# A sliding-window attention stage on one Trainium2 core: another way to the inverse norms, product runs in halves, and a new order on all engines

## What is computed

```
for i in range(6):                                   # DEPTH
    x = attn_layer(shift_tokens(x), ...) + x
    x = ffn_layer(shift_tokens(x), ...) + x
attn_layer:
    q, k, v = split(x @ Wqkv)                        # 16 heads of 64
    q = l2norm(q) * q_scale;  k = l2norm(k) * k_scale   # t / max(norm(t), 1e-12)
    q, k = rotary(q), rotary(k)                      # with tables of cosine, sine and scale
    sim = 8 * q k^T over windows of 32 and the window before, masked
    out = softmax(sim) @ v;  return out @ Wo
ffn_layer:
    xn = (x - mean) / sqrt(var + 1e-5) * g + b
    a, gate = split(xn @ W1 + b1)                    # 2 x 341
    return a * gelu(gate) @ W2 + b2
```

## Time and profile before

| | |
|---|---|
| median of three executions | 5155.24 us (5143.06 to 5160.82) |
| span of the profiled execution | 5148.7 us; its own device time is not listed apart and lies among those of the runs |
| TensorE | busy 4508.2 us, 88% |
| VectorE | busy 3456.9 us, 67% |
| GpSimd | busy 3075.1 us, 60% |
| ScalarE | busy 2317.0 us, 45% |
| mean granted TensorE clock | 0.910 over the span, 1.00 in the deep stage |

### The profile page before, as it was taken

One profiled execution on the slowest core, in us unless ns is written; L12 is line 12 of the kernel. 1 busy time (PEld: TensorE's weight loads), 2 busy tenths in 40 slices (PEclk: granted clock), 3 DMA queues, 4 the chain that ended last, 5 costly groups with the idle time before them and its releaser, 6 DMA issues.

```text
span 5148.7 us, 147111 instructions
## 1 busy us (share of the span) xinstructions
PE 4508.2 (88%) x66028; PEld 2555.2 (50%) x66028; DVE 3456.9 (67%) x4153; ACT 2317.0 (45%) x2523; POOL 3075.1 (60%) x1713
## 2 busy tenths in 40 slices
PE   6898689977468999999999999568999999999998
PEld 3444333333135555555555555235555555555554
DVE  4365536632437778778777776447877787888885
ACT  1242134433134555555555555234555555555553
POOL 0010000000019889888889997049988899998984
PEclk7699679976569999999999999669999999999999
DMA  2000000000001112111111111101111111112111
GB/s 71 1 1 1 0 0 1 1 0 0 0 22 32 30 29 55 29 51 32 52 29 53 31 29 33 44 9 29 33 51 30 35 49 30 54 29 55 30 32 29
DMA packets 78094, 144.43 MB, mean 28 GB/s; under 512 B 18728, under 2 KB 24944, under 8 KB 75824
## 3 DMA queue, kind: packets, MB, share of 16 engines
q1 hardware_dynamic: 77488, 135.23, 10.1%
HBM read 39.75 MB, written 1.05 MB: 8 GB/s over the span
## 4 chain that ended last, share of the span: by engine, by line
PE 47%; issue 23%; POOL 21%; DVE 7%; ACT 1%; DMA 0%; SPq 0%; DVEq 0%; POOLq 0%
POOL arena L1446 8%; PE psum L1033 8%; POOL arena L1439 6%; POOL arena L1452 5%; PE psum L1050 4%; PE psum L1064 4%; PE psum L1102 4%; PE psum L1083 4%; PE psum L1002 3%; PE psum L1148 3%; PE psum L1097 2%; PE psum L1142 2%; PE psum L524 2%; POOL rstd L1457 2%; PE psum L1016 2%
## 5 line engine op out<-in xcount | busy, mean ns | idle before, releaser
L1446 POOL TENSOR_TENSOR arena<-arena,minus_half 128x16 f32<-128x16 f32 x384 | 1131.9, 2948 | 32.0
L1439 POOL TENSOR_TENSOR arena<-arena 128x1024 f32<-128x1024 f32 x384 | 909.8, 2369 | 13.5 <-DVE arena L1324 13.5
L1452 POOL TENSOR_TENSOR arena<-arena 128x1024 f32<-128x1024 f32 x384 | 733.7, 1911 | 42.6
L1320 DVE TENSOR_TENSOR arena<-psum,arena 128x1024 f32<-128x1024 f32 x384 | 468.1, 1219 | 404.1 <-ACT arena L1202 404.1
L1462 POOL MEMSET arena<- 128x33 f32 x4 | 0.4, 128 | 995.3 <-DVE std L1686 995.3
L1208 ACT ACTIVATE arena<-psum 128x1024 f32<-128x1024 f32 x384 | 392.2, 1021 | 298.8 <-PE psum L1050 298.4
L1202 ACT ACTIVATE arena<-psum 128x1024 f32<-128x1024 f32 x384 | 392.3, 1022 | 246.5 <-PE psum L1033 243.4
L1324 DVE TENSOR_TENSOR arena<-psum,arena 128x1024 f32<-128x1024 f32 x384 | 466.8, 1215 | 54.1 <-PE psum L1050 54.1
L1050 PEld LDWEIGHTS psum<-w_ident,arena 128*128 128x128 f32 x3072 | 355.3, 141 | 281.9 <-issue 148.5
L1331 DVE TENSOR_REDUCE arena<-arena 128x16 f32<-128x1024 f32 x384 | 464.8, 1211 | 2.8
L1235 ACT ACTIVATE arena<-psum 128x1024 f32<-128x1024 f32 x192 | 196.7, 1024 | 580.7 <-PE psum L1064 580.7
(11 more groups left out here) (260 smaller groups left out, 7703.9 us busy)
## 6 DMA issues: line engine op xcount, KB each, us to landing
arena<-arena SPq DMA_DIRECT2D x672, 128.0 KB, 2.3
deep_wqkv<-in_deep_wqkv SPq DMA_DIRECT2D x6, 1536.0 KB, 7.1
arena<-in_deep_wqkv SPq DMA_DIRECT2D x6, 1536.0 KB, 7.2
arena<-arena SPq DMA_DIRECT2D x96, 64.0 KB, 2.5
deep_wo<-in_deep_wo SPq DMA_DIRECT2D x6, 512.0 KB, 7.5
arena<-in_deep_wo SPq DMA_DIRECT2D x6, 512.0 KB, 7.4
deep_w<-in_deep_w SPq DMA_DIRECT2D x6, 341.0 KB, 7.6
arena<-in_deep_w SPq DMA_DIRECT2D x6, 341.0 KB, 7.5
```

Source lines behind the costliest of these rows:

```text
L1320: nc.vector.tensor_tensor(turned[:, hs, :].rearrange("p h (a e) -> p h a e", a=2), swapped, sin, ALU.mult).then_inc(de.deep_rope_parts, 1)
L1439: nc.gpsimd.tensor_tensor(roped[:, hs, :], roped[:, hs, :], turned[:, hs, :], ALU.add).then_inc(de.deep_summed, 1)
L1446: nc.gpsimd.tensor_tensor(h_inv[a % 2][:, hs], h_inv[a % 2][:, hs], minus_half[:, :], ALU.pow).then_inc(de.deep_inv_ready, 1)
L1452: nc.gpsimd.tensor_tensor(roped[:, hs, :], roped[:, hs, :], over(h_inv[a % 2][:, hs], [P, LHEADS, LD]), ALU.mult).then_inc(de.deep_roped, 1)
```

## The change

It replaces the power on GpSimd: VectorE clamps the sums of squares of q and k together (128x32) and takes the reciprocal, ScalarE takes the square root one step later, and GpSimd scales both halves in that step. `roped` gets two buffers, and `qT` becomes two buffers of one tile. The scores' run of short products is cut in two halves with the value product between them, the mix in two halves with the second turn between them. The lists of all four engines get a new order. The division of the probabilities stays on VectorE, now behind the second half's parts in three of four steps. The diff, with the renaming of buffers and unchanged waits left out:

```diff
--- before.py
+++ after.py
@@ -944,18 +944,19 @@
-        qT = new(PAIRS, T)
+        qT = [new(PAIRS, P) for _ in range(2)]
...
-        roped = new(2 * LHEADS, LD)
+        roped = [new(2 * LHEADS, LD) for _ in range(2)]
...
-        h_sum, h_inv = [new(2 * LHEADS) for _ in range(2)], [new(2 * LHEADS) for _ in range(2)]
+        h_sum, h_low, h_rcp = (new(2 * LHEADS) for _ in range(3))
+        h_inv = [new(2 * LHEADS) for _ in range(2)]
@@ -982,7 +983,7 @@
-        def scores_pe(pe, c, j):
+        def scores_open_pe(pe, c, j):
@@ -995,15 +996,23 @@
-            for pair in range(PAIRS):
+            scores_pe(j, 0)
...
+        def scores_close_pe(pe, c, j):
+            scores_pe(j, 1).then_inc(de.deep_scores_ready, 1)
...
+        def scores_pe(j, part):
...
+            t = j % TILES
+            for pair in range(PAIRS // 2 * part, PAIRS // 2 * (part + 1)):
...
-                                                qT[r64, pair, wi * WIN:(wi + 1) * WIN],
+                                                qT[j % 2][r64, pair, jj * WIN:(jj + 1) * WIN],
...
-            last.then_inc(de.deep_scores_ready, 1)
+            return last
@@ -1037,25 +1046,19 @@
         def turn_pe(pe, c, a, half):
...
-            if half == 1 and a >= 1:
+            if half == 1:
+                pe.wait_ge(de.deep_turn_kept, 2 * i + 1)
+            elif a >= 1:
...
-            elif half == 1:
-                pe.wait_ge(de.deep_turn_kept, 2 * i + 1)
-            elif a >= 2:
-                pe.wait_ge(de.deep_probs_kept, i - 1)
-            elif a == 1:
-                pe.wait_ge(de.deep_turn_kept, 2 * i)
...
-                last = nc.tensor.matmul(turns[:, m * P:(m + 1) * P], roped[:, h:h + 2, :], w.ident[:, :], start=True, stop=True,
+                last = nc.tensor.matmul(turns[:, m * P:(m + 1) * P], roped[a % 2][:, h:h + 2, :], w.ident[:, :], start=True, stop=True,
...
         def value_pe(pe, c, a):
...
-            if a + 1 < ALL:
-                pe.wait_ge(de.deep_turn_kept, 2 * i + 3)
-            else:
+            if a >= 1:
@@ -1065,7 +1068,7 @@
-        def mix_pe(pe, c, j):
+        def mix_open_pe(pe, c, j):
@@ -1073,7 +1076,15 @@
-            for pair in range(0, PAIRS, 2):
+            mix_pe(j, 0)
...
+        def mix_close_pe(pe, c, j):
+            mix_pe(j, 1).then_inc(de.deep_pv_done, 1)
...
+        def mix_pe(j, part):
...
+            t = j % TILES
+            for pair in range(PAIRS // 2 * part, PAIRS // 2 * (part + 1), 2):
@@ -1083,7 +1094,7 @@
-            last.then_inc(de.deep_pv_done, 1)
+            return last
@@ -1154,37 +1165,39 @@
                 ending, begun = 0 <= n - 2 < UNITS, 0 <= n - 1 < UNITS
                 if s < ALL:
                     qk_pe(pe, c, s, 0)
+                if 0 <= s - 2 < ALL:
+                    scores_open_pe(pe, c, s - 2)
+                    value_pe(pe, c, s - 2)
+                    scores_close_pe(pe, c, s - 2)
                 if t == 0 and ending:
-                    mean_pe(pe, c, n - 2)
+                    var_pe(pe, c, n - 2)
                 if t == 1 and ending:
                     gate_pe(pe, c, n - 2, 0)
+                if t == 2 and ending:
+                    a_pe(pe, c, n - 2, 2)
+                if t == 3 and begun:
+                    wo_rest_pe(pe, c, n - 1)
+                if s < ALL:
+                    qk_pe(pe, c, s, 1)
                 if 0 <= s - 1 < ALL:
                     turn_pe(pe, c, s - 1, 0)
-                if 0 <= s - 2 < ALL:
-                    scores_pe(pe, c, s - 2)
-                if t == 2 and ending:
-                    a_pe(pe, c, n - 2, 2)
-                if 0 <= s - 2 < ALL:
-                    value_pe(pe, c, s - 2)
-                if t == 0 and ending:
-                    var_pe(pe, c, n - 2)
-                if s < ALL:
-                    qk_pe(pe, c, s, 1)
-                if t == 3 and begun:
-                    wo_rest_pe(pe, c, n - 1)
+                if 0 <= s - 3 < ALL:
+                    mix_open_pe(pe, c, s - 3)
                 if t == 1 and ending:
                     gate_pe(pe, c, n - 2, 1)
                 if 0 <= s - 1 < ALL:
                     turn_pe(pe, c, s - 1, 1)
+                if t == 3 and begun:
+                    mean_pe(pe, c, n - 1)
                 if 0 <= s - 3 < ALL:
-                    mix_pe(pe, c, s - 3)
+                    mix_close_pe(pe, c, s - 3)
+                if t == 0 and ending:
+                    spread_pe(pe, c, n - 2)
                 if t == 1 and ending:
                     gate_pe(pe, c, n - 2, 2)
                     a_pe(pe, c, n - 2, 0)
                 if t == 2 and ending:
                     down_pe(pe, c, n - 2)
-                if t == 0 and ending:
-                    spread_pe(pe, c, n - 2)
                 if t == 2 and begun:
                     wo_first_pe(pe, c, n - 1)
                 if 0 <= s - 2 < ALL:
@@ -1201,10 +1214,17 @@
+        def norms_act(act, c, a):
+            i = c * ALL + a
+            act.wait_ge(de.deep_sq_inv, i + 1)
+            if a >= 2:
+                act.wait_ge(de.deep_roped, 2 * i - 2)
+            nc.scalar.activation(h_inv[a % 2], h_rcp, ACT.Sqrt).then_inc(de.deep_inv_ready, 1)
...
         def turn_act(act, c, a, half):
...
-            dst = kT[:, :, WIN + t * P:WIN + (t + 1) * P] if half else qT[:, :, t * P:(t + 1) * P]
+            dst = kT[:, :, WIN + t * P:WIN + (t + 1) * P] if half else qT[a % 2]
@@ -1262,7 +1282,7 @@
                 if s < ALL:
                     square_act(act, c, s, 0)
                 if 0 <= s - 1 < ALL:
-                    turn_act(act, c, s - 1, 0)
+                    norms_act(act, c, s - 1)
                 if t == 0 and ending:
                     ln_square_act(act, c, n - 2)
                 if 0 <= s - 2 < ALL:
@@ -1270,6 +1290,8 @@
+                if 0 <= s - 1 < ALL:
+                    turn_act(act, c, s - 1, 0)
@@ -1319,16 +1341,25 @@
-            if a >= 1:
-                dve.wait_ge(de.deep_turned, 2 * i - 1 + half)
-            nc.vector.tensor_tensor(roped[:, hs, :], qk_half, under(tabs[:, 2 * half, t, :], shape),
+            if a >= 2:
+                dve.wait_ge(de.deep_turned, 2 * i - 3 + half)
+            nc.vector.tensor_tensor(roped[a % 2][:, hs, :], qk_half, under(tabs[:, 2 * half, t, :], shape),
...
         def squares_dve(dve, c, a, half):
...
-            if a >= 2:
-                dve.wait_ge(de.deep_inv_ready, 2 * i - 3 + half)
-            nc.vector.tensor_reduce(h_sum[a % 2][:, hs], qk_sq[:, hs, :], AX.X, ALU.add).then_inc(de.deep_sq_summed, 1)
+            if a >= 1:
+                dve.wait_ge(de.deep_clamped, i)
+            nc.vector.tensor_reduce(h_sum[:, hs], qk_sq[:, hs, :], AX.X, ALU.add).then_inc(de.deep_sq_summed, 1)
...
+        def norms_dve(dve, c, a):
+            i = c * ALL + a
+            dve.wait_ge(de.deep_sq_summed, 2 * i + 2)
+            nc.vector.tensor_scalar(h_low, h_sum, NORM_FLOOR, None, ALU.max).then_inc(de.deep_clamped, 1)
+            dve.wait_ge(de.deep_clamped, i + 1)
+            if a >= 1:
+                dve.wait_ge(de.deep_inv_ready, i)
+            nc.vector.reciprocal(h_rcp, h_low).then_inc(de.deep_sq_inv, 1)
@@ -1388,38 +1419,39 @@
             for s in range(LAST + 1):
                 n, t = s // TILES, s % TILES
                 ending, begun = 0 <= n - 2 < UNITS, 0 <= n - 1 < UNITS
+                if t == 0 and ending:
+                    centre_dve(dve, c, n - 2)
+                if t == 2 and ending:
+                    hidden_dve(dve, c, n - 2, 1)
                 if t == 3 and ending:
                     end_dve(dve, c, n - 2)
                 if s < ALL:
                     parts_dve(dve, c, s, 0)
                 if 0 <= s - 2 < ALL:
                     max_dve(dve, c, s - 2)
-                if t == 2 and ending:
-                    hidden_dve(dve, c, n - 2, 1)
-                if 0 <= s - 2 < ALL:
                     less_max_dve(dve, c, s - 2)
+                if t == 0 and ending:
+                    var_dve(dve, c, n - 2)
                 if s < ALL:
                     squares_dve(dve, c, s, 0)
                 if t == 2 and ending:
                     hidden_dve(dve, c, n - 2, 2)
+                if t == 3 and begun:
+                    attn_dve(dve, c, n - 1)
+                if s < ALL and t != 3:
+                    parts_dve(dve, c, s, 1)
                 if 0 <= s - 2 < ALL:
                     row_sum_dve(dve, c, s - 2)
-                if t == 0 and ending:
-                    var_dve(dve, c, n - 2)
-                if 0 <= s - 2 < ALL:
                     divide_dve(dve, c, s - 2)
+                if s < ALL and t == 3:
+                    parts_dve(dve, c, s, 1)
                 if s < ALL:
-                    parts_dve(dve, c, s, 1)
-                if t == 2 and 2 <= n + 1 < UNITS:
-                    shift_dve(dve, c, n + 1)
+                    squares_dve(dve, c, s, 1)
+                    norms_dve(dve, c, s)
```

(36 more changed lines are left out.)

## The result

The changed kernel takes 5282.47 us (5277.36 to 5288.05) against 5154.27: ratio **1.0243, 95% interval 1.0221 to 1.0266**. It is slower, as forecast; the loss is 128 us where 77 were forecast, and 5282 lies at the upper edge of the forecast's own range (5184 to 5280). The profiled execution has 5277.36 us and a span of 5275.6.

What follows compares the result with a forecast made beforehand. The new order's loop through the late division, late scale and TensorE's work were to set steps of 17.1+18.5+19.0+17.0 = 71.6 us a unit against 70.0. Over 48 units that adds 77: 5148.7+77+6.5 = 5232 us, range 5040 to 5330.

Steps and rivals of the forecast that it cites:

- loop: From q/k product through VectorE's late division and the probabilities' transposes to the next q/k product: 16.1 us a step.
- collision: VectorE's division meets GpSimd's second add in three of four steps and ends at 15.8 instead of 15.0 us.
- the norm's power: First step, GpSimd: layer norm's power of four columns, taken as 2 us, ahead of the adds; second add ends at 15.0.
- about 14: Length in us a step of the same chain in the old order, with the division before the second parts.
- The late scale and affine: Second step: the affine waits for VectorE's layer norm scale and heads ScalarE's queue, moving the square and what follows by 1.0 us.
- Table loads: ScalarE: nine loads of 1.28 us a unit instead of two, hidden in idle time with 0.8 us to spare.
- the halves of scores and mix cost nothing I can see: TensorE: cutting both runs in halves was priced at zero.
- 2.1 us of gaps: TensorE: gaps inside score and mix runs, 2.1 us a unit, taken as gone with the halves.
- GpSimd: Without powers and clamps it keeps two adds and two scales, about 9 us busy a step, and stops being a bound.
- (1): Division not caught by GpSimd's add: unit 69.6 us, -19 us, 5136 us; chance 0.15.
- (2): TensorE becomes the bound, decided at the probabilities' transposes in the first two steps: unit 67, -144 us, 5011; chance 0.15.
- (3): ScalarE's table switches reach the path at 2.6 us each: unit 75.8, +278 us, 5433; chance 0.08.

Runs made afterwards that it cites:

- e1: Changed kernel with row sum, reciprocal and division ahead of the second half's parts in every step: ratio 1.0123 to the kernel before, 5217 us.
- e2: Changed kernel with GpSimd's second add of a step waiting until the same step's division is done: ratio 1.0168 to the kernel before.
- e5: Changed kernel with the layer norm's scale moved ahead of the square sum and norms on VectorE: ratio 1.0193 to the kernel before, 5249 us.
- e3: Changed kernel with a copy in place of the norms' square root, so no table switch for it: ratio 1.0253 to the kernel before.
- e4: Changed kernel with the scores' two halves next to each other again, ahead of the value product: ratio 1.0153 to the kernel before.
- e7: Changed kernel with both halves of the mix ahead of the second turn: ratio 1.0236 to the kernel before.
- e8: Changed kernel with division ahead of second parts, layer norm's scale earlier and whole mix ahead of second turn: ratio 0.9804 to the kernel before, 5043 us.
- e11: Kernel before with its scores cut in halves around the value product: ratio 1.0108 to the kernel before, 5207 us.
- e10: Changed kernel with division ahead of second parts and the layer norm's scale earlier, both runs still in halves: ratio 0.9881 to the kernel before, 5091 us.
- e6: Kernel before with row sum, reciprocal and division behind the second half's parts in three of four steps: ratio 1.0015 to the kernel before.
- e12: Changed kernel with division first, scale earlier, mix whole, and clamp and power back on GpSimd, 128x32 at once: ratio 1.0186 to the kernel before, 5250 us.

## Why the prediction was right, and where not

Direction, loop and collision were right; the size was short by 51 us.

**The loop** was right in place and, within 0.2 us, in its links: 16.1 forecast plus the collision, 17.0 measured. e1 takes it away (first step 15.1), and e2 prices the collision at 0.9 us, the 0.8 of the text. That the first step came out at 17.1 is in part luck. The text let the norm's power, taken as 2 us, hold the adds up until 15.0. It takes 1.02 and holds up nothing that counts; the second add waits for the parts, which end 0.2 later than said because the cut scores delay the max, and it ends at 14.9. The two errors cancel. That the old order would close in "about 14" was not reached: in e1's first step 0.84 us are the second transposes' wait for the copy of the first, and the rest, 14.3, is TensorE's own work, where the sum had 13.5.

**The late scale and affine** in the second step were right: 1.0 us said, 0.7 found by e5. What I did not see is that this wait grows when the first step gets shorter (e1: from 11 to 95 us, e2: to 61), so that e1 and e2 alone each paid some 40% of what their texts said.

**Table loads**: hidden, as said, with 1.06 us to spare in the second step above. Rows of after and e3 agree with 1.28 us and no more. The Trainium skill, "ScalarE: Activation LUTs", "What ACT_TABLE_LOAD costs", counts some 1.38 us of drain besides; the root starts 0.01 us behind its load's end, and here the measurement decides.

**The step that failed** is a term put at nothing, "the halves of scores and mix cost nothing I can see", and beside it some prices of issue. Missing are 1.1 us a unit (72.7 against 71.6), 0.3 of them in the third step and 0.7 in the fourth. e4 measures the scores' cut: 46 us in time, 39 of them between the first and last scales of the two calls, and in the stretch of the steps 0.3 in the third and 0.2 in the fourth step. That covers the third. The rest of the fourth, 0.6 us, stays with the scores whole (17.6) and with the mix whole (17.8), so it is not the halves. Pieces of the fourth step in the changed kernel's chain, and one group of transposes behind a wait from the chain of the kernel before:

```profile
4245.19 4.49 PE psum L1113 x10
...
4253.52 1.06 PE psum L1055 x8
...
4256.50 1.02 PE psum L1025 x8
...
4210.04 1.09 PE psum L1050 x8
```

The sum had 4.29, 0.87 and 0.87 for the first three, 0.5 us less in all. It took each from one place of the old chain and used it at another place of the new one, with another neighbour or behind a wait; the last row shows that the old chain had the higher price too, in transposes that had waited for GpSimd. Whether the mix's cut has a price of its own isn't shown: e7 and e8 move its second half as well as joining it.

The gain set against the halves, 2.1 us of gaps, I counted as gone, and they were. What that was worth no run here isolates: in e11 the step that held the gap did get shorter, and other waits and the clock took more than that back.

**GpSimd** at 9 us a step: 599/1200x18.2 = 9.1. **VectorE**: reciprocal 0.353 against 0.35 taken. The clamp had no price of its own; its mean is 0.49, and it lies ahead of a wait, so it cost nothing, as said.

**Rivals.** (1) divisions at 1.23: not so, mean 1.84; between 3600 and 4800 us 50 of 66 take 2.1 and 16 take 1.2, three of four steps and the fourth, as said. (2) TensorE the bound: not so in this order; e8, with another order and 67.6 us a unit, is close to the 67 it described. (3) loads on the path: not so.

## What to carry to other kernels

When a bound is taken away, draw the next loop at once: follow one tile from product to product through every queue, and ask which instruction at the end of the step waits for it; here undoing the late division and the late scale together gave 187 us (e10 against the changed kernel), while in the old order the late division cost nothing, since other waits and gaps shrank by as much (e6). Cures for waits that follow each other don't simply add: e1 and e5 gave 1.2% and 0.5% alone, 3.6% together, so try them in pairs. A cut into halves has a price that a list of busy times doesn't show: what is issued in between delays whoever waits for the end of the run (e4). And look at the granted clock of the stage in every run: in e7 and e12 a part of the loss is a clock that fell behind a longer wait, not work or waiting that the sum could hold.

## What the runs showed of the hardware that I had not expected

The clamp on VectorE, 128x32 with one input in SBUF, takes 0.18 us when GpSimd rests (49 of 66 between 3600 and 4800 us) and 1.31 or 1.32 when it begins inside GpSimd's add (the other 17); it then ends with the add. The sum of squares just ahead of it, also one input in SBUF, runs in 1.21 beside the same add. From the timeline of the changed kernel:

```profile
4256.41 1.21 DVE L1353 TENSOR_REDUCE arena<-arena 128x16 f32<-128x1024 f32 x1
...
4256.57 2.36 POOL L1471 TENSOR_TENSOR arena<-arena 128x1024 f32<-128x1024 f32 x1 [6.21 <-DVE arena L1346]
...
4257.65 1.31 DVE L1358 TENSOR_SCALAR arena<-arena 128x32 f32<-128x32 f32 x1
```

GpSimd's power of 128x32 takes 5.48 us against 2.95 for 128x16: some 0.16 us a column and 0.4 besides (an estimate from the two). The layer norm's power of four columns takes 1.02 in the changed kernel; in the kernel before its median is 2.00, and there it starts while a division runs on VectorE. The other way round the power is harmless: 18 divisions of the kernel before between 3600 and 4800 us lie inside a power of 128x16, and each takes 1.22 or 1.23, where one inside an add took 3.32.
